# Scores of a key tile in four PSUM banks with one exponential; attention output summed in SBUF

## The reference

```python
def _L0_attn_ref(x, Mq, Mk, Mv):           # 8 heads of 64, value heads of 128, C = 2048
    q = (x @ Mq).reshape(B, H, C, K)
    k = (x @ Mk).reshape(B, H, C, K)
    v = (x @ Mv).reshape(B, H, C, V)
    scores = jnp.einsum('bhqk,bhck->bhqc', q, k).reshape(B * H, C, C)
    att = jax.nn.softmax(scores / jnp.sqrt(jnp.float32(K)), axis=1)
    att4 = att.reshape(B, C, H, C)
    out = jnp.einsum('bqhc,bhcd->bqhd', att4, v)
    return out.reshape(B, C, H * V)
def _L0_ffn_ref(x, w_gate, w_up, w_down):  # int32 weights, SCALE = 1/127, hidden 3072
    gate = jnp.einsum('bsd,hd->bsh', x, wg)
    up = jnp.einsum('bsd,hd->bsh', x, wu)
    h = jax.nn.silu(gate) * up
    return jnp.einsum('bsh,dh->bsd', h, wd)
x = x + _layernorm(_L0_attn_ref(_layernorm(x, axis=-1), L0_attn_Mq, L0_attn_Mk, L0_attn_Mv), axis=-1)
x = x + _layernorm(_L0_ffn_ref(_layernorm(x, axis=-1), L0_ffn_w_gate, L0_ffn_w_up, L0_ffn_w_down), axis=-1)
```

## Time and profile before

| | us |
|---|---|
| three executions | 1762.24, 1765.6, 1766.82; median 1765.6 |
| profiled execution | 1772.76, of which the span is 1771.0 (core 4, the slowest) |
| spans of the eight cores | 1747.3 to 1771.0 |
| TensorE busy in the span | 1693.3 (96%) |
| VectorE, ScalarE busy | 849.6, 854.0 |

### The profile page before, as it was taken

One profiled execution on the slowest core, in us unless ns is written; L12 is line 12 of the kernel. 1 busy time (PEld: TensorE's weight loads), 2 busy tenths in 40 slices (PEclk: granted clock), 3 DMA queues, 4 the chain that ended last, 5 costly groups with the idle time before them and its releaser, 6 DMA issues.

```text
span 1771.0 us, 31869 instructions; the slowest of 8 cores (1747.3 to 1771.0 us)
## 1 busy us (share of the span) xinstructions
PE 1693.3 (96%) x10912; PEld 799.9 (45%) x10912; DVE 849.6 (48%) x1904; ACT 854.0 (48%) x1447; POOL 125.9 (7%) x245
## 2 busy tenths in 40 slices
PE   5999986998999999999999999999999999999997
PEld 2444442444444444444444444444444444444443
...
GB/s 197 198 201 253 222 224 150 214 189 240 258 123 142 190 159 132 129 199 155 143 114 199 154 159 102 194 150 174 85 185 176 173 93 170 158 162 48 155 95 48
DMA packets 157518, 288.35 MB, mean 163 GB/s; under 512 B 56624, under 2 KB 75056, under 8 KB 156976
## 3 DMA queue, kind: packets, MB, share of 16 engines
...
...
## 4 chain that ended last, share of the span: by engine, by line
PE 83%; DVE 6%; DMA 5%; issue 2%; ACT 2%; SPq 1%; POOL 1%; DVEq 0%; POOLq 0%; ACTq 0%
PE F L71 58%; PE Op L71 17%; PE Sp L71 8%; DMA xnT<-xn 2%; DVE bnB L225 1%; DVE bnB L226 1%; DMA wgu<-gu_bf 1%; DMA wk<-mk 1%; ACT E L419 1%; ACT y L244 1%; SPq L78 1%; DMA wd_sb<-wd 1%; DVE th L528 1%; DMA xl<-x 0%; DVE mvB L227 0%
## 5 line engine op out<-in xcount | busy, mean ns | idle before, releaser
L419 ACT ACTIVATE E<-Sp 128x1024 bf16<-128x1024 f32 x512 | 523.8, 1023 | 625.9 <-PE Sp L71 625.7
L71 PE MATMUL F<-x2T,wgu 128*128 128x512 bf16 x3072 | 780.0, 380 | 20.3 <-DVE th L528 16.1
L71 PEld LDWEIGHTS F<-x2T,wgu 128*128 128x128 bf16 x3072 | 256.8, 98 | 307.6 <-issue 109.0
L71 PE MATMUL F<-wd_sb,hT 128*128 128x512 bf16 x1536 | 365.7, 380 | 0.7 <-DMA wd_sb<-wd 0.5
L71 PEld LDWEIGHTS Op<-vt,E 128*128 128x128 bf16 x4096 | 270.9, 98 | 122.5 <-issue 7.8
L71 PE MATMUL Op<-vt,E 128*128 128x128 bf16 x4096 | 313.7, 220 | 0.8 <-DVE vt L429 0.8
L528 DVE SCALAR_TENSOR_TENSOR th<-th,F 128x512 f32<-128x512 f32 x192 | 131.9, 687 | 259.8 <-ACT th L524 259.8
L551 DVE TENSOR_TENSOR hT<-th,F 128x512 bf16<-128x512 f32 x192 | 131.8, 686 | 180.1 <-PE F L71 176.2
L71 PEld LDWEIGHTS F<-wd_sb,hT 128*128 128x128 bf16 x1536 | 137.7, 98 | 157.3 <-issue 23.9
L71 PE MATMUL Sp<-qk 64*128 64x512 bf16 x1024 | 200.1, 387 | 2.4 <-ACT E L419 1.5
L429 DVE TENSOR_SCALAR vt<-vt,rsx 128x1024 bf16<-128x1024 bf16 x256 | 125.4, 490 | 53.9 <-DVE rsx L428 45.9
...
## 6 DMA issues: line engine op xcount, KB each, us to landing
wgu<-gu_bf SPq DMA_DIRECT2D x192, 512.0 KB, 4.2
vt<-v_d SPq DMA_DIRECT2D x256, 256.0 KB, 4.6
xl<-x SPq DMA_DIRECT2D x32, 512.0 KB, 9.0
x<-x SPq DMA_DIRECT2D x32, 512.0 KB, 5.9
out<-x SPq DMA_DIRECT2D x32, 512.0 KB, 2.7
...
v_d<-vst SPq DMA_DIRECT2D x16, 512.0 KB, 12.0
```

What stands on the lines that cost most here:

```text
L71: "tensor", lambda t: t.matmul(out, lhsT, rhs, start=start, stop=stop),
L419: lambda s: s.activation(e[:, 1024 * c:1024 * (c + 1)], Sp[:, :], AF.Exp, scale=0.125, accum_out=accx[:, a:a + 1]), done, av_tok.get(K - 4))
```

## The change

A key tile's scores are now one unit: four matmuls into the four-bank tile `S`, in the same order as before (rows 0 to 63, rows 64 to 127, then both again for the second half), and one exponential over 2048 columns, whose sum needs no addition. The side list has the slots S, av, av, empty. Output is accumulated over four key tiles (a quarter of a group) for one half of the columns at a time, in two banks `O`. Each quarter and half is then unloaded: the first quarter of a group is copied to `y2` (one half by ScalarE, one by VectorE), the other three are added to it by VectorE. The matmuls' count and shapes are unchanged. With it go:

- value tiles are loaded and scaled by column halves (512 transfers of 128 KB, 12 buffers), the second half's scale being due later; `E` is one tile with four and six slots for the two halves;
- normalisation after attention works on half tiles, with its first statistics taken per half and the scales due 2.0 and 4.0 after it, where they were due 5.0 and 7.0 after the last unload;
- `qk_d` holds no swapped copy of the keys; `load_qk` makes it with two further transfers;
- 9 `convert` transfers are left, at other places; hidden tiles 18 to 23 are loaded in block 0 as int32 through the GpSimd queue into the weight buffers, used, and stored to `gu_bf` from there (`keep_wgu`);
- one `th` buffer instead of two, `LEAD` 8, `SPACE` 3.0; some tiles move in SBUF (x1 4 to 7 and x2T1 lie over tiles of the projections and wait for their end, `ramp_idle`).

```diff
-LAG = 2
-LEAD = 6.0
+LEAD = 8.0
 QUIET = 5
 MM = 0.216
-SPACE = 1.6
+SPACE = 3.0
+CONV = 18
...
+    E = sb("E", [128, 10 * 1024], BF16)
+    vt = [sb(f"vt{i}", [128, 512], BF16) for i in range(12)]
...
-    Op = [pt(f"Op{i}", [128, 1024], F32) for i in range(2)]
+    O = [pt(f"O{i}", [128, 512], F32) for i in range(2)]
+    F = [pt(f"F{i}", [128, 512], F32) for i in range(2)]
-    Sp = pt("Sp", [128, 1024], F32)
+    S = pt("S", [128, 2048], F32)
...
-                row = 2 * blk * 128 * 3072
...
+                row = 2 * blk * 128 * 2048 + 1024 * which
+                qk_stored[blk] = P.dma(
+                    "sync", bass.AP(qk_d.tensor, row, [[2048, 128], [128 * 2048, 2], [1, 1024]]),
+                    bass.AP(st, 0, [[2048, 128], [1024, 2], [1, 1024]]), q_qks[blk], *ev)
...
+        buf, ready = qk[G % 2], [qk_stored[G // 2], s_done.get(16 * (G - 2) + 15)]
+        P.dma("sync", buf[:, 0:2048], qk_d[G, :, :], q_qk[G % 2], *ready)
+        for lo in (0, 64):
+            qk_tok[G] = P.dma("sync", buf[lo:lo + 64, 2048:3072], qk_d[G, 64 - lo:128 - lo, 1024:2048],
+                              q_qk[G % 2], *ready)
+    def v_slot(K, c):
+        return 6 * c + K % 6
+    def load_v(K, c):
+        b, t, i = K // 128, K % 16, v_slot(K, c)
         stored = [v_stored[4 * b + 2 + p, h] for p in range(2) for h in range(2)]
-        v_tok[K] = P.dma("sync", vt[K % 6][:, :], v_d[16 * b + t, :, :], q_v[K % 6],
-                         *stored, av_tok.get(K - 6))
+        v_tok[K, c] = P.dma("sync", vt[i][:, :], v_d[16 * b + t, :, 512 * c:512 * (c + 1)], q_v[i],
+                            *stored, av_tok[K - 6, c] if K >= 6 else None)
...
+    def s_unit(K):
         G, t = K // 16, K % 16
         s_at[0] = P.now
-        if c == 0 and t == 0 and G + 1 < 16:
+        if t == 0 and G + 1 < 16:
             load_qk(G + 1)
+        if t == 12:
+            load_x1(2 * G)
+            load_x1(2 * G + 1)
...
-        free = exp_tok.get((K, 0)) if c else exp_tok.get((K - 1, 1))
...
+        for c in range(2):
+            waits = [exp_tok.get(K - 1), qk_tok[G], *s_first] if c == 0 else ()
+            P.mm(S[:, 1024 * c:1024 * c + 512], buf[0:64, own + col:own + col + 128],
+                 buf[0:64, 512 * c:512 * (c + 1)], True, True, waits)
+            done = P.mm(S[:, 1024 * c + 512:1024 * c + 1024], buf[64:128, other + col:other + col + 128],
+                        buf[64:128, 512 * c:512 * (c + 1)], True, True, done=c == 1)
         s_first.clear()
-        done = P.mm(Sp[:, 512:1024], buf[64:128, other + col:other + col + 128],
...
+        s_done[K] = done
+        to = bass.AP(E, 1024 * (K % 4), [[10240, 128], [1024 * (4 + K % 6 - K % 4), 2], [1, 1024]])
+        exp_tok[K] = P.act(
+            lambda s: s.activation(to, S[:, :], AF.Exp, scale=0.125, accum_out=accx[:, K % 16:K % 16 + 1]),
+            done, av_tok[K - 4, 0] if K >= 4 else None, av_tok[K - 6, 1] if K >= 6 else None)
+        P.later(2.5, lambda: v_scale(K, 0))
+        P.later(5.5, lambda: v_scale(K, 1))
+    def v_scale(K, c):
+        r, v_ = rsx[:, K % 16:K % 16 + 1], vt[v_slot(K, c)]
+        if c == 0:
+            rs_tok[K] = P.dve(lambda v: v.reciprocal(r, accx[:, K % 16:K % 16 + 1]), exp_tok[K])
+        vs_tok[K, c] = P.dve(lambda v: v.tensor_scalar(v_[:, :], v_[:, :], r, None, AL.mult),
+                             rs_tok[K], v_tok[K, c])
+    def av_unit(K, c):
+        v_, j = vt[v_slot(K, c)], K % 4
+        base = 1024 * (4 + K % 6 if c else K % 4)
+        for h in range(4):
+            col = base + 512 * (h % 2) + 256 * (h // 2)
             for d in range(2):
                 waits = []
-                if h % 4 == 0 and d == 0:
...
+                if h == 0 and d == 0:
+                    waits = [vs_tok[K, c]] + (o_free if j == 0 else [])
+                tok = P.mm(O[d][:, 128 * h:128 * (h + 1)], E[:, col + 128 * d:col + 128 * (d + 1)],
+                           v_[:, 128 * h:128 * (h + 1)], j == 0 and h == 0, j == 3 and h == 3,
+                           waits, done=h == 3 and d == 1)
+        av_tok[K, c] = tok
+        if K + 6 < NKT:
+            load_v(K + 6, c)
+        if j == 3:
+            unload(K // 4, c, tok)
+    def unload(Q, c, done):
+        G, u = Q // 4, 2 * (Q // 4) + c
+        y = y2[u % 3]
+        ev = []
+        for d in range(2):
+            part = y[:, 512 * d:512 * (d + 1)]
+            if Q % 4:
+                t = P.dve(lambda v, d=d, part=part: v.tensor_tensor(part, part, O[d][:, :], AL.add),
+                          done, y2_tok[u, d])
+            elif d == 0:
+                t = P.act(lambda a, d=d, part=part: a.copy(part, O[d][:, :]), done, y2_tok.get((u - 3, d)))
+            else:
+                t = P.dve(lambda v, d=d, part=part: v.tensor_copy(part, O[d][:, :]), done,
+                          y2_tok.get((u - 3, d)))
+            y2_tok[u, d] = t
+            ev.append(t)
+        o_free[:] = ev
+        if Q % 4 == 3:
+            P.later(1.5, lambda: half_stats(G, c))
+    def half_stats(G, c):
+        u, a = 2 * G + c, 2 * (G % 2)
+        y = y2[u % 3]
+        for d in range(2):
+            o = 12 * (a + d) + 6 * c
+            P.dve(lambda v, d=d, o=o: v.bn_stats(bnB[:, o:o + 6], y[:, 512 * d:512 * (d + 1)]), y2_tok[u, d])
+        if c:
+            ln2(G)
...
+        ready, shift, x1_done, scaled = {}, {}, {}, {}
+        for d in range(2):
+            s = a + d
+            ready[d] = ln_rstd(bnB, mvB, vfB, rsB, s, EPS, ("c_vector", P.count["c_vector"]))
+            shift[d] = ln_shift(mvB, rsB, nbB, s, ready[d])
...
+            s = a + d
+            for c in range(2):
+                part = y2[(2 * G + c) % 3][:, 512 * d:512 * (d + 1)]
+                scaled[d, c] = P.act(lambda e, part=part: e.activation(
+                    part, part, AF.Identity, bias=nbB[:, s:s + 1], scale=rsB[:, s:s + 1]), shift[d])
+            P.later(1.2, lambda: residual(d))
+        def residual(d):
+            xt = x1[(2 * G + d) % 8]
+            for c in range(2):
+                u = 2 * G + c
+                x1_done[d] = y2_tok[u, d] = P.dve(lambda v, c=c, u=u: v.tensor_tensor(
+                    xt[:, 512 * c:512 * (c + 1)], xt[:, 512 * c:512 * (c + 1)],
+                    y2[u % 3][:, 512 * d:512 * (d + 1)], AL.add), scaled[d, c], x1_tok[2 * G + d])
             if d:
-                ln2_done[G] = [x1_done[0], x1_done[1]]
                 P.later(0.5, stats3)
...
-        P.later(1.5, stats)
...
+                x2T_tok[n] = P.flip(dst, x2[d][:, :], q_x2T[4 * (blk % 2) + jj], t,
+                                    *([up_done[blk - 2]] if blk >= 2 else ramp_idle if blk else ()))
+        P.later(2.0, lambda: scale(0))
+        P.later(4.0, lambda: scale(1))
...
-        wgu_tok[i] = P.dma("sync", wgu[i % 4][:, :], gu_bf[ht, :, :], q_wgu[i % 4],
-                           conv_tok[ht // 2], wgu_read.get(i - 4), *(xl_idle if i < 4 else ()))
+        spill = [conv_tok[i - 4]] if CONV <= i - 4 < NHT else []
+        if CONV <= i < NHT:
+            wgu_tok[i] = P.dma("gpsimd", wgu[i % 4][:, :], gu_hbm[ht, :, :], q_wgc[i % 4],
+                               wgu_read[i - 4], *spill)
+        else:
+            wgu_tok[i] = P.dma("sync", wgu[i % 4][:, :], gu_bf[ht, :, :], q_wgu[i % 4],
+                               conv_tok[ht], wgu_read.get(i - 4), *spill, *(xl_idle if i < 4 else ()))
+    def keep_wgu(i):
+        conv_tok[i] = P.dma("sync", gu_bf[i, :, :], wgu[i % 4][:, :], q_keep[i], wgu_tok[i])
...
-        t_ = th[i % 2]
+        t_ = th
         tanh = P.act(lambda s: s.activation(t_[:, :], F[0][:, :], AF.Tanh, scale=1.0 / 254.0),
-                     done, th_read.get(i - 2), *(th_idle if i < 2 else ()))
+                     done, th_read[i - 1] if i else None, *(() if i else th_idle))
+        if CONV <= i < NHT:
+            keep_wgu(i)
...
-    side = [("s", K, c) for K in range(LAG) for c in range(2)]
...
+    side = []
+    for K in range(NKT + 3):
+        side.append(("s", K, 0) if K < NKT else None)
+        Q, c = ((K // 4, 0), (K // 4 - 1, 0), (K // 4 - 1, 1), (K // 4 - 1, 1))[(K + 1) % 4]
+        lo = 4 * Q + 2 * (K % 4 in (0, 2))
+        side += [("av", lo, c), ("av", lo + 1, c)] if Q >= 0 else [None, None]
+        side.append(None)
     side_at = [0]
     def run_side(upto):
         while side_at[0] < min(upto, len(side)):
-            kind, K, c = side[side_at[0]]
...
+            unit = side[side_at[0]]
+            if unit and unit[0] == "s":
+                if P.now - s_at[0] < SPACE and upto - side_at[0] < 6:
+                    return
+                s_unit(unit[1])
+                P.tick(0.64)
+            elif unit:
+                av_unit(*unit[1:])
+                P.tick(0.45)
             side_at[0] += 1
-            P.tick(0.42 if kind == "s" else 0.45)
...
-    early_conv = {22: 0, 30: 1, 40: 2, 50: 3}
-    later_conv = {(4, 12): 4, (5, 6): 5, (6, 0): 6, (6, 6): 7, (6, 12): 8, (7, 2): 9}
```

(4 more changed lines are left out.)

156 lines of the change are left out of this document (36 added, 120 removed).

## The result

The changed kernel takes 1794.0 us (median of three executions, 1791.7 to 1798.7), the kernel before 1764.3 beside it (four executions): a ratio of 1.0165, slower by 1.7%; the 95% interval of the ratio is [1.0131, 1.0200]. The forecast was 1738, range 1712 to 1774.

A forecast was written before the change was run, and what follows sets the result against it. TensorE itself was taken as the limit. Terms summed to -34.3 us from 1772.8, giving 1738.5; from the median 1765.6 the transposing term shrank from 12 to 5, again 1738. Range 1712 to 1774.

The forecast's parts named there:

- the stream: TensorE's work: one score unit saves 0.21 us per key tile, 0.14 in gate and up cycles: -22.7, -11.3 and -8.4 us.
- Rival C: Score unit: an exposed weight load makes the second score pair dearer by 0.10 us, giving 1766 us; chance 0.16.
- the quiet gate and up cycle: Feed-forward gate and up pairs: cycle falls from 5.21 to 5.07 us, set by the gate chain; -22.7 us over 162 cycles.
- the down cycle: Down units: cycle of 6.93 us falls to 6.72, the full 0.21 saved; -11.3 us over 54 cycles.
- VectorE's work: VectorE over the whole kernel: busy time rises from 850 to some 960 us, mainly for more output unloads.
- the transposing wait: Projection stage: 12 of a 17.3 us stall on a transposing transfer goes; 5 when counted from the median shown.
- normalisation, +9.1: Normalisation inside gate and up cycles, once per block: 3.9 us against 2.6, 7 blocks, +9.1 us (0 to +25).
- the value halves, +5: Value loads by halves: one key tile in four has 6.7 us in the projection stage; late ones cost +5 us (0 to +33).
- rival D: Projection stage and block 0: late value halves hold VectorE, 33 us instead of 5, giving 1775 us; chance 0.14.
- Nothing is lost, with little to spare: VectorE's order in a quiet cycle: its added unloads fit, with 0.45 us of slack for a fresh output accumulation.
- The tie: Gate and up cycle: gate chain 5.07 us against TensorE's own 5.00, only 0.07 us apart.
- the weight waits priced at +6: Block 0: six hidden tiles loaded as int32 and stored back, beside already late `wd` loads: +6 us (-4 to +20).

The follow-up runs named there:

- e16: Changed kernel with the second value half's scale due at 12.0 instead of 5.5 and LEAD 8.25 instead of 8, nine converts kept: ratio 0.9908 to the kernel before.
- e5: Changed kernel with LEAD 8.25, the second value half's scale due at 12.0 and the twelve converts of before: 1740.0 us, ratio 0.9847.
- e13: Changed kernel without value-half loads from the seventh key tile on, so its result is wrong: 1755.5 us, ratio 0.9939 to the kernel before.
- e14: Kernel before without value-tile loads from the seventh key tile on, as a control: 1752.0 us, ratio 0.9913 to the kernel before.
- e3: Changed kernel with LEAD 8.25 instead of 8, every slot half a unit earlier: 1762.9 us, ratio 0.9957 to the kernel before.
- e10: Kernel before with LEAD 6.25 instead of 6.0: ratio 1.0122 to the unedited kernel before.
- e2: Changed kernel with the weights' conversion of before, twelve converts and no int32 loads in block 0: ratio 1.0126 to the kernel before.
- the spread: Second tile's normalisation one gate/up pair later, first tile's statistics directly behind its residual sum; on the changed kernel: 1763.4 us, ratio 0.9994 to the kernel before.

## Why the prediction was wrong

Against the mean spans the forecast, with 5 for the transposes, is -27.3 us: -42.4 for the stream, +15.1 of waits, nothing for the clock. Measured are -44.9, +46.3 and +19.7, together +21.1. So the miss of 48.4 us is 31.2 of waits and 19.7 of clock, less 2.5 of the stream.

**Right: the stream.** The second score pair costs its streaming time: unit 0.54 us before the next F, saving 0.21. Rival C, by the rule of the Trainium skill, "TensorE: Matmul & The Clock Gate", section on packing small matmuls, would show 0.65; the trace doesn't agree with it. The exponential (1.876 for 1.87), the quiet gate and up cycle (5.05 for 5.07), the down cycle (exponentials at 705.47 and 712.18: 6.71 for 6.72) and VectorE's work (948.5 for 960) all came.

**Right: the transposing wait.** It is gone (mean 0.2 us, 4.5 before), and by the fewer converts (e16 against e5). The 12 us of the earlier trace rows were those of the slowest core; the 5 that the median was given fits the mean.

**Right: normalisation, +9.1.** Counted were 3.9 us a block for 2.6, of which 0.65 and 2.8 stay at two products. The two waits at 1182.04 and 1190.10 are 0.69 and 2.90. Over 560 to 1500 us, some five blocks, waits on the product rose from 10.9 to 17.7 (means), 1.3 a block as forecast.

**Wrong: the value halves, +5.** "For one key tile in four the second half's scale follows two cycles later, 6.7 us": the room and the halves that lack it were right. The landing was wrong: it was taken from a median, 10.5 us, with half the bytes as an argument for less. The four second halves of the table took 20.6 to 26.8 us from the free buffer to the landing, 11.0 to 19.8 of it behind the issue, though the medians of the stretches are only 4.5 to 9.2. VectorE waited 60.5 us nine times, 16.4 at the longest, and TensorE's waits on value scales went from 0.9 to 24 (mean). In its sign this is rival D, given 0.14 and 33 us; e13 against e14 puts it at 19 to 25, with the clock in it. D's own count did not come: ten halves late by 3.8 us were expected in the projection stage, and two or three on each core were late by 7 to 17. (In its block 0 the room of two cycles is 2 x 5.07 - 1.5 = 8.6, not 8.8, which changes D by 1 us.)

**Wrong: "Nothing is lost, with little to spare".** The order of VectorE's list was worked out for a quiet cycle alone, which left 0.45 us of slack for a copy of `O` and 0.2 for F1. In the cycles with a normalisation the copy stands behind it: TensorE's waits on O<-DVE y went from nothing to 9.2 us up to 530 and 5.5 from 560 to 1500, and those on `hT`, held by the residual sum of the block before (765.28 to 766.50 on core 6), from nothing to 3.3. That is 18 us for a term put at nothing, and it is what makes the steady waits rise by 15.0, where the product alone gives 7.

**Missing: the clock.** No term and no rival had it. The kernel before lost nothing between 530 and 1560 us, with no wait over 1.7 us there, so nothing in its late part hinted at a price; in its projections and block 0 it lost 3.4. After the change the clock costs 19.7 us more in all.

**The tie.** The 0.07 us between chain and stream was called little. e3 and e10 show what a slot is worth: it moves either kernel by 20 to 37 us, in opposite directions.

**Luck.** Block 0 grew by 5.9, for about 4 from its terms (6 + 1.3 - 24 x 0.14). But the weight waits priced at +6 did not rise (6.7 us before, 6.0 after, means). What came was the half (62, 1), late behind the stores of those weights, 6.3 us of TensorE's time on core 6.

**Still open.** Why the stream of e3 is 12.0 us shorter, when the cycle's 0.06 explains 9.7; why e2 gave half of what its waits promised; why a half takes 17 us to land. The single `th` buffer, the two further transfers of `load_qk` and the moved tiles were not tested alone; the stream leaves no room for a cost of theirs, the waits do. Whether the kernel before gains from the spread was not tried.
